# Score tiles of three attention layers laid out by source, from broadcast rows

## The chip, the cores and the metric

The kernel runs on one core of one Trainium2 chip. The metric is the device time of one execution in microseconds, lower is better; a quoted time is the median of a few runs. TensorE (PE) multiplies matrices and writes PSUM; VectorE (DVE), ScalarE (ACT) and GpSimd (POOL) work on elements; each engine runs its own instructions in order and they wait for each other on semaphores.

## The reference

Four graph networks run one after another over 625 nodes with 768 features, each followed by a residual layer norm: an RGCN (three layers), a GCN (two), a GAT with 4 heads and then 1, and a GAT with 8 heads of 96 features and then 1. What matters here is the attention layer, computed for each head:

```python
h = (x @ W).reshape(n, heads, out_c)
al_s = jnp.einsum('nhc,hc->nh', h, a_src)
al_d = jnp.einsum('nhc,hc->nh', h, a_dst)
e = jax.nn.leaky_relu(al_s[src] + al_d[dst], 0.2)
m = jax.ops.segment_max(e, dst, num_segments=n)
ex = jnp.exp(e - m[dst])
z = jax.ops.segment_sum(ex, dst, num_segments=n)
alpha = ex / (z[dst] + 1e-16)
out = jax.ops.segment_sum(h[src] * alpha[:, :, None], dst, num_segments=n)
```

## The kernel before, in words

The graph is held dense: a 625 x 625 table of edge counts in five blocks of 125 nodes (NB = 5, BP = 125). For a head, the exponent of an edge from s to d is the larger of two sums, a steep one al_s + al_d - m and a flat one 0.2 al_s + 0.2 al_d - m; m is the largest score of destination d. The four attention layers are Q0 (4 heads, a residual product beside it), Q1 (1 head, a residual product), Q2 (8 heads) and Q3 (1 head). The order of the work on each engine is written out by hand.

Each layer starts with its feature product x @ W on TensorE in chunks (`first_piece`, then `chunks_and_scores`, which calls `chunk_step` L2387 once a step and puts the score work between the steps by the table `rows_at` and `turned_at`). `early_scores` and `turn_scores` give al_s and al_d of all heads. Then, for each head:

- TensorE broadcasts al_s as one row to 125 partitions of PSUM (`send_row`, matmuls at L2457), and ScalarE copies it, times 0.8, to SBUF (`keep_row`, L1075).
- VectorE finds m for five blocks of destinations (`largest`, L1815; it waits for the copy) and makes two columns a block (`columns`, L1824 to L1827), destinations on the partitions.
- VectorE makes a 125 x 625 tile with destinations on the partitions, max(0.8 al_s + row_steep, row_flat), by `steep_or_flat` (L1885), one for each block of destinations.
- TensorE turns the five 125 x 125 blocks of the tile into PSUM (`turn_tile`, L2475), four blocks to a bank; ScalarE takes exp in place with 0.2 al_s as bias (`exps`, L1087); VectorE caps at 1 and multiplies by the counts (`probs`, L1848).
- TensorE sums the features of the sources with these blocks as stationary operand (`sum_unit`, L2486); the last column of the features is one and gives z.

In Q2 the loop runs over 40 tiles (head, block of destinations): TensorE turns tile j + 2, sums tile j and sends the row of head h + 2 when the block is 0. After a head VectorE scales its output by 1 / z and adds the bias (`head_read`, L1963 and L1967), ScalarE takes exp for the elu (`elu_exp`, L1244) and VectorE finishes the elu (`head_elu`, L1973, L1974). In Q1 four of five tiles are turned between chunk steps 4 to 7. In Q3 they are turned after the chunks. The weight chunks of the next product are split in two parts by ScalarE (L1065) and GpSimd (L766) on the way.

Of the kernel before, what the change touches and what calls it, by code (L numbers as in the profile page):

```python
# [5 lines left out]
F32 = mybir.dt.float32  # L6
# [67 lines left out]
class Attention:  # L74


    def __init__(self, before, heads, c, k, pieces, residual, chunk, loops, rows, turned, kept):
# [32 lines left out]
        self.rows_at, self.turned_at, self.kept_after = rows, turned, kept  # L110
# [15 lines left out]
        self.p_ring = {0: 4, 1: 5, 2: 6, 3: 5}[self.index]  # L126
        self.g_ring = {0: 2, 1: 3, 2: 3, 3: 3}[self.index]
# [65 lines left out]
class Memory:  # L193


    def __init__(self, nc):
# [56 lines left out]
        def edge(name, shape, dt, offset):  # L253
# [107 lines left out]
def program(nc, x, src, dst, etype, weights, rgcn_bias, gcn_bias, vec, out):  # L361
    ctx = ExitStack()
    with ctx:
# [167 lines left out]
        cols_ready = sem("cols_ready")  # L531
        g_ready = sem("g_ready")
# [32 lines left out]
        def kept_row(q, h):  # L565

            return mem.tiles[0:BP, 1 + h % 4, :]

        def g_tile(q, j):

            return mem.tiles[0:BP, {0: 5, 1: 2, 2: 5, 3: 2}[q.index] + j % q.g_ring, :]

        def p_tile(q, j):

            i = j % q.p_ring
            if q.index == 0:
                return mem.tiles[0:BP, (7, 8, 9, 0)[i], :]
            if q.index == 2:
                return mem.more[0:BP, i, :]
            return mem.tiles[0:BP, 5 + i, :]  # L580
# [111 lines left out]
        def _(pool):  # L692
# [174 lines left out]
            split_to(Q2.chunk + 15)  # L867
            split_to(Q2.end + AHEAD)
# [9 lines left out]
        def _(act):  # L878
# [190 lines left out]
            def keep_row(q, h):  # L1069

                act.wait_ge(row_sent, q.head0 + h + 1)
                if h >= 4:
                    act.wait_ge(g_ready, q.tile0 + (h - 3) * NB)
                a = row_col(q)
                nc.scalar.activation(kept_row(q, h), ps[0:BP, a:a + N], ACT.Copy, scale=1.0 - SLOPE).then_inc(row_kept, 1)  # L1075
# [15 lines left out]
            def feature_product(q):  # L1091
                n = len(q.pieces)
                for g, bank_ in enumerate(q.banks[0:NB * n]):
# [25 lines left out]
                    if m == NB - 1 and piece in q.kept_after:  # L1119
                        for step, heads, tiles in q.kept_after[piece]:  # L1120
                            split_hi(q.chunk + q.k + step + 7)
                            for h in heads:
                                keep_row(q, h)
                            exps(q, tiles)
# [93 lines left out]
            exps(Q1, NB)  # L1218
# [27 lines left out]
            for j in range(len(Q2.tiles)):  # L1246
                h, b = Q2.tiles[j]
                split_hi(min(chunks_split[0] + 1, Q2.end + AHEAD))
                exps(Q2, min(j + 3, len(Q2.tiles)))
                if b == 0 and h + 2 < Q2.heads:  # L1250
                    keep_row(Q2, h + 2)
                if b == 3 and h:
                    elu_exp(h - 1)
            elu_exp(Q2.heads - 1)
# [4 lines left out]
            exps(Q3, NB)  # L1259
# [8 lines left out]
        def _(dve):  # L1268
# [527 lines left out]
            def scores_begin(q):  # L1796
# [5 lines left out]
                                             ALU.mult))  # L1802
                if q.index + 1 < len(LAYERS):
                    scores_split(q.index + 1)

            def largest(q, h, m):

                mask = mem.mask_loop if q.loops else mem.mask_plain
                if m == 0:
                    dve.wait_ge(row_kept, q.head0 + h + 1)  # L1810
# [40 lines left out]

            def inverse(z, sums, guard):
# [25 lines left out]
            def steep_or_flat(q, j):  # L1878

                h, b = q.tiles[j]  # L1880
                dve.wait_ge(cols_ready, q.head0 + h + 1)
                dve.wait_ge(row_kept, q.head0 + h + 1)
                if j >= q.g_ring:
                    dve.wait_ge(g_turned, (q.tile0 + j - q.g_ring + 1) * NB)
                nc.vector.tensor_scalar(g_tile(q, j), kept_row(q, h), mem.row1[0:BP, b, h:h + 1], mem.row2[0:BP, b, h:h + 1],  # L1885
# [804 lines left out]
```

## Time and profile before

| what | us |
|---|---|
| median of 3 runs | 1610.96 (1610.59 to 1614.87) |
| profiled execution | 1607.97 |
| its span | 1606.2 |
| PE busy | 1464.7 (91%) |
| DVE busy | 791.7 (49%) |
| ACT busy | 427.4 (27%) |
| POOL busy | 506.6 (32%) |

The span is from the first to the last instruction in the trace. Times in the rows are counted from its start. The attention layers begin near 1000 us: Q1's scores stand at 1212 to 1248, Q2's at 1353 to 1506, Q3's at 1534 to 1594.

### The profile page before, as it was taken

The numbers are of one execution on the slowest core, as the hardware profiler recorded it, in microseconds if no ns is written. First come the engines' busy times: TensorE is split into PE (matmuls) and PEld (weight loads), VectorE is DVE, ScalarE is ACT, GpSimd is POOL, SyncE is SP. The second block draws the span as 40 slices with busy tenths as digits, with TensorE's granted clock in tenths as the row PEclk, the third lists the DMA queues.
The fourth block names the chain that finished last, engine by engine and source line by source line (L and its number), as shares of the span: only waits on it lengthen the run. The fifth ranks groups of instructions, "written<-read, shape, count | busy, mean of one in ns | idle before, by whom it ended". The sixth has DMA issues, their size and how long they took to land.

```text
span 1606.2 us, 23414 instructions
## 1 busy us (share of the span) xinstructions
PE 1464.7 (91%) x8072; PEld 1343.7 (84%) x8072; DVE 791.7 (49%) x1940; ACT 427.4 (27%) x1009; POOL 506.6 (32%) x586
## 2 busy tenths in 40 slices
PE   5899699999999999999999998999688998878896
PEld 3566699999999999999998997898578867767773
DVE  7889644224443365642324435534534043678524
ACT  1153511111000001101003113345524333544422
POOL 5110332423334424434342420633226534100020
PEclk9999899999999999999999998999889999777998
DMA  3110111213343243422112211310012102000001
GB/s 113 41 30 9 37 45 30 60 32 82 89 132 105 63 116 84 123 74 60 55 50 59 60 30 41 87 58 26 20 47 81 49 5 84 16 1 1 10 1 48
DMA packets 57656, 86.53 MB, mean 54 GB/s; under 512 B 6442, under 2 KB 54183, under 8 KB 57433
## 3 DMA queue, kind: packets, MB, share of 16 engines
q1 hardware_dynamic: 45184, 66.02, 14.3%
q10 hardware_dynamic: 12374, 19.17, 4.1%
q8 instruction: 66, 1.08, 0.3%
q14 instruction: 32, 0.26, 0.1%
HBM read 83.24 MB, written 1.92 MB: 53 GB/s over the span
## 4 chain that ended last, share of the span: by engine, by line
PE 74%; DVE 14%; ACT 5%; issue 4%; POOL 1%; DMA 1%; DVEq 0%; ACTq 0%; SPq 0%; POOLq 0%
PE psum L2060 13%; PE psum L2064 12%; PE psum L2063 12%; PE psum L2486 7%; PE psum L2077 7%; PE psum L2080 7%; PE psum L2165 2%; PE psum L2401 1%; PE psum L2406 1%; PE psum L2405 1%; ACT psum L1087 1%; DVE onehot_dst L1370 1%; PE psum L2121 1%; PE psum L2475 1%; PE psum L2457 1%
## 5 line engine op out<-in xcount | busy, mean ns | idle before, releaser
L2060 PE MATMUL psum<-w_lo,xT_hi 128*125 128x384 f32 (+2 forms) x1200 | 412.1, 343 | 11.7 <-POOL w_lo L766 5.3
L2063 PE MATMUL psum<-w_hi,xT_lo 128*125 128x384 f32 (+2 forms) x1200 | 405.5, 338 | 0.0
L2064 PE MATMUL psum<-w_hi,xT_hi 128*125 128x384 f32 (+2 forms) x1200 | 405.0, 337 | 0.0
L753 POOL CAST w_hi<-w_raw 128x384 fp32r<-128x384 f32 x190 | 103.3, 544 | 502.4 <-PE psum L2064 492.3
L2060 PEld LDWEIGHTS psum<-w_lo,xT_hi 128*125 128x125 f32 (+1 forms) x1200 | 225.0, 187 | 16.5 <-POOL w_lo L766 8.3
L766 POOL TENSOR_TENSOR w_lo<-w_raw,w_hi 128x384 fp32r<-128x384 f32 x106 | 109.8, 1065 | 387.9 <-ACT w_hi L1065 277.1
L2063 PEld LDWEIGHTS psum<-w_hi,xT_lo 128*125 128x125 f32 (+1 forms) x1200 | 225.4, 188 | 0.1
L2064 PEld LDWEIGHTS psum<-w_hi,xT_hi 128*125 128x125 f32 (+1 forms) x1200 | 224.8, 187 | 0.0
L1406 DVE TENSOR_TENSOR h_lo<-psum,h_hi 125x384 fp32r<-125x384 f32 (+1 forms) x120 | 66.9, 558 | 316.1 <-ACT h_hi L923 315.1
L2077 PE MATMUL psum<-h_lo,adjacency 125*125 125x384 f32 (+3 forms) x600 | 204.1, 340 | 1.8 <-ACT adjacency L963 1.7
L755 POOL TENSOR_TENSOR w_lo<-w_raw,w_hi 128x384 fp32r<-128x384 f32 x190 | 200.8, 1057 | 15.2
L923 ACT ACTIVATE h_hi<-psum 125x384 fp32r<-125x384 f32 (+1 forms) x120 | 59.0, 491 | 545.3 <-PE psum L2064 540.9
L2080 PE MATMUL psum<-h_hi,adjacency 125*125 125x384 f32 (+3 forms) x600 | 203.4, 339 | 0.0
L2486 PE MATMUL psum<-features,score_tiles 125*125 125x257 f32 (+2 forms) x400 | 122.6, 461 | 4.4 <-DVEq L2012 3.1
L2077 PEld LDWEIGHTS psum<-h_lo,adjacency 125*125 125x125 f32 (+1 forms) x600 | 112.0, 187 | 3.2 <-ACT adjacency L963 2.3
L1087 ACT ACTIVATE psum<-psum,al_src_slope 125x125 f32<-125x125 f32 x350 | 94.7, 351 | 73.9 <-PE psum L2475 73.8
L2080 PEld LDWEIGHTS psum<-h_hi,adjacency 125*125 125x125 f32 (+1 forms) x600 | 112.5, 188 | 0.3
L2486 PEld LDWEIGHTS psum<-features,score_tiles 125*125 125x125 f32 x400 | 79.2, 202 | 36.6 <-issue 5.0
L2486 PE MATMUL psum<-features,more_tiles 125*125 125x97 f32 x400 | 68.5, 334 | 26.1 <-DVE more_tiles L1848 25.9
L2486 PEld LDWEIGHTS psum<-features,more_tiles 125*125 125x125 f32 x400 | 63.5, 246 | 30.1 <-DVE more_tiles L1848 30.0
L2165 PE MATMUL psum<-onehot_dst,onehot_src 128*125 128x512 bf16 x336 | 62.5, 326 | 6.3 <-DVE onehot_dst L1370 5.9
L1370 DVE TENSOR_SCALAR onehot_dst<-iota,dst_of_pair 128x625 bf16<-128x625 f16 x168 | 62.8, 410 | 9.7 <-PE psum L2165 9.7
(286 smaller groups left out, 2097.9 us busy)
## 6 DMA issues: line engine op xcount, KB each, us to landing
w_raw<-weights_dram SPq DMA_DIRECT2D x296, 192.0 KB, 2.4
score_w_raw<-weights_dram ACTq DMA_DIRECT2D x58, 192.0 KB, 2.9
x_nat<-x_dram SPq DMA_DIRECT2D x1, 1875.0 KB
x_residual<-x_dram SPq DMA_DIRECT2D x1, 1875.0 KB
out_dram<-x_residual SPq DMA_DIRECT2D x5, 375.0 KB
score_a_rows<-L_gnn_a_src_dram ACTq DMA_DIRECT2D x8, 192.0 KB, 3.4
score_a_rows<-L_gnn_a_dst_dram ACTq DMA_DIRECT2D x8, 192.0 KB, 5.1
rgcn_bias<-rgcn_bias_dram SPq DMA_DIRECT2D x1, 1125.0 KB
```

Source lines behind the costliest of these rows:

```text
L753: nc.gpsimd.tensor_copy(mem.wh[:, slot, :], mem.raw[:, raw_slot, :]).then_inc(w_hi_ready, 1)
L755: nc.gpsimd.tensor_tensor(mem.wl[:, slot, :], mem.raw[:, raw_slot, :], mem.wh[:, slot, :].bitcast(F32), ALU.subtract).then_inc(w_lo_ready, 1)
L766: nc.gpsimd.tensor_tensor(mem.wl[:, c % WRING, :], mem.raw[:, c % RAW, :], mem.wh[:, c % WRING, :].bitcast(F32), ALU.subtract).then_inc(w_ ...
L1087: ins = nc.scalar.activation(t, t, ACT.Exp, bias=mem.al_src2[0:BP, n % NB, h:h + 1])
L1370: nc.vector.tensor_scalar(mem.oh_dst[:, n % OH_RING, 0:N], mem.iota[:, 0:N], mem.dst_pair[:, s % 2, j:j + 1], None, ALU.is_equal).then_inc ...
L2060: ins = nc.tensor.matmul(o, h, wl, start=(j == 0), stop=False, skip_group_check=True)
L2063: nc.tensor.matmul(o, l, wh, start=False, stop=False, skip_group_check=True)
L2064: ins = nc.tensor.matmul(o, h, wh, start=False, stop=stop and j == k - 1, skip_group_check=True)
L2077: ins = nc.tensor.matmul(o, a, mem.hl[0:p, slot, 0:width], start=(s == 0), stop=False, skip_group_check=True)
L2080: ins = nc.tensor.matmul(o, a, mem.hh[0:p, slot, 0:width], start=False, stop=(s == NB - 1), skip_group_check=True)
L2165: ins = nc.tensor.matmul(o, mem.oh_src[:, t, 0:BP], mem.oh_dst[:, n % OH_RING, w:w + 512 if w == 0 else NC], start=False, stop=(t == GROUP ...
L2486: ins = nc.tensor.matmul(bank(q.out_bank(u), off, off + width), blocks(p_tile(q, j))[:, k, :], feat_flat(q, k, a, a + width), start=(k == ...
```

## The change

Q0 stays as it is. In Q1, Q2 and Q3 the tiles have sources on the partitions and destinations along the free dimension, so that no block has to be turned. What changes:

- `keep_row` is gone in these layers; `largest` waits for the row in PSUM.
- `turn_columns`: after `columns`, TensorE turns the two columns of each of five blocks (125 x 2) into two rows of 625 in PSUM. `keep_columns`: ScalarE copies the two rows to SBUF in two instructions.
- `send_columns`: TensorE broadcasts the flat row and then the steep row to 125 partitions of PSUM, 2 x 2 pieces. `keep_flat`: ScalarE copies the flat one to SBUF.
- `score`: VectorE makes each of five 125 x 625 tiles as max(steep row + 0.8 al_s, flat row) with the steep row in PSUM and the flat one in SBUF. `source_exps`: ScalarE takes exp of a whole tile in SBUF. `finish`: VectorE caps at 1 and multiplies by the counts, all in SBUF.
- `sum_head` (Q2): all five tiles of a head are used together, 25 blocks of 97 columns, as each tile becomes ready.
- In Q2, scaling a head's output by 1 / z goes to ScalarE (five instructions on 96 columns) and adding the bias to GpSimd; the loop runs over heads and TensorE's order in it is `turn_columns(h+1)`, `send_columns(h+1)`, `send_row(h+2)`, `sum_head(h)`. The turn stands before chunk step 3 and the send before step 4 in all three layers; the row of head 1 of Q2 moves from step 4 to step 5 and waits for head 0's tiles to be scored, since it shares their bank. GpSimd splits one weight chunk fewer before Q2's heads.

The core of the diff:

```diff
 Q1 = Attention(Q0, 1, D, K8, PIECES, True, BASE_L2B, True,
-               {1: (0,)}, {4: 0, 5: 1, 6: 2, 7: 3}, {0: ((1, (0,), 0), (5, (), 2), (7, (), 4))})
+               {1: (0,)}, {3: ("turn", 0), 4: ("send", 0)}, {0: ((3, (0,), 0), (6, (), NB))})
 Q2 = Attention(Q1, HEADS3, C3, KC, PIECES, False, BASE_L3, False,
-               {1: (0,), 4: (1,)}, {}, {0: ((1, (0,), 0), (4, (1,), 0))})
+               {1: (0,), 5: (1,)}, {3: ("turn", 0), 4: ("send", 0)}, {0: ((3, (0,), 0), (4, (), NB))})
 Q3 = Attention(Q2, 1, D, KC, PIECES, False, BASE_L3 + 2 * KC, False,
-               {1: (0,)}, {}, {0: ((1, (0,), 0),)})
+               {1: (0,)}, {3: ("turn", 0), 4: ("send", 0)}, {0: ((3, (0,), 0), (4, (), NB))})
...
+            def keep_columns(q, h):
+                act.wait_ge(cols_turned, q.head0 + h - HEADS2 + 1)
+                if q.by_head and h >= 2:
+                    act.wait_ge(pair_sent, q.head0 + h - HEADS2 - 1)
                 a = row_col(q)
-                nc.scalar.activation(kept_row(q, h), ps[0:BP, a:a + N], ACT.Copy, scale=1.0 - SLOPE).then_inc(row_kept, 1)
+                nc.scalar.activation(kept_columns(h)[:, 0:4 * BP], ps[0:2, a:a + 4 * BP], ACT.Copy)
+                nc.scalar.activation(kept_columns(h)[:, 4 * BP:N], ps[0:2, a + 512:a + 512 + BP], ACT.Copy).then_inc(cols_kept, 1)
+            def keep_flat(q, h):
+                if apart(q, h):
+                    act.wait_ge(flat_sent, h)
+                else:
+                    act.wait_ge(pair_sent, q.head0 + h - HEADS2 + 1)
+                a = pair_col(q, h, 1)
+                nc.scalar.activation(flat_row(h), ps[0:BP, a:a + N], ACT.Copy).then_inc(flat_kept, 1)
+            def source_exps(q, h):
+                for k in range(NB):
+                    t = source_tile(q, h, k)
+                    act.wait_ge(tile_scored, scored(q, h, k))
+                    nc.scalar.activation(t, t, ACT.Exp, bias=mem.al_src2[0:BP, k, h:h + 1]).then_inc(tile_exp, 1)
...
+            for h in range(HEADS3):
+                if h + 1 < HEADS3:
+                    keep_columns(Q2, h + 1)
+                    keep_flat(Q2, h + 1)
+                if h:
+                    head_read(h - 1)
+                if h + 1 < HEADS3:
+                    source_exps(Q2, h + 1)
+                if h:
                     elu_exp(h - 1)
...
+            def score(q, h, k):
+                if k == 0:
+                    dve.wait_ge(pair_sent, q.head0 + h - HEADS2 + 1)
+                    dve.wait_ge(flat_kept, q.head0 + h - HEADS2 + 1)
+                    if q.by_head and h >= 2:
+                        dve.wait_ge(part_done, q.unit0 + h - 1)
+                nc.vector.scalar_tensor_tensor(source_tile(q, h, k), steep_row(q, h), mem.al_steep[0:BP, k, h:h + 1], flat_row(h),
+                                               ALU.add, ALU.max).then_inc(tile_scored, 1)
+            def finish(q, h, k):
+                cnt, t = mem.cnt_loop if q.loops else mem.ctot, source_tile(q, h, k)
+                dve.wait_ge(tile_exp, scored(q, h, k))
+                nc.vector.scalar_tensor_tensor(t, t, 1.0, cnt[0:BP, k, 0:N], ALU.min, ALU.mult).then_inc(tile_ready, 1)
...
+            scores_of(Q2, 0)
+            for k in range(NB):
+                score(Q2, 0, k)
+            for h in range(HEADS3):
+                if h + 1 < HEADS3:
+                    scores_of(Q2, h + 1)
+                for k in range(NB):
+                    finish(Q2, h, k)
+                if h:
+                    head_z(h - 1)
+                if h >= 2:
+                    head_elu(h - 2)
+                if h + 1 < HEADS3:
+                    for k in range(NB):
+                        score(Q2, h + 1, k)
...
+            scores_of(Q3, 0)
+            for step in (score, finish):
+                for k in range(NB):
+                    step(Q3, 0, k)
...
+            def turn_columns(q, h):
+                pe.wait_ge(cols_ready, q.head0 + h + 1)
+                for m in range(NB):
+                    a = row_col(q) + (m * BP if m < NB - 1 else 512)
+                    ins = nc.tensor.transpose(ps[0:2, a:a + BP], mem.row12[0:BP, :, m, h], mem.ident[0:BP, 0:BP])
+                ins.then_inc(cols_turned, 1)
+            def send_columns(q, h):
+                pe.wait_ge(cols_kept, q.head0 + h - HEADS2 + 1)
+                if h:
+                    pe.wait_ge(tile_scored, scored(q, h - 1, NB - 1))
+                    if h == 1:
+                        pe.wait_ge(gemm_read, q.gemm0 + NB + 2)
+                for i in (1, 0):
+                    for p, e, a, z in score_pieces(pair_col(q, h, i)):
+                        ins = nc.tensor.matmul(ps[0:BP, p:e], mem.ident[0:2, i:i + 1].to_broadcast([2, BP]),
+                                               kept_columns(h)[:, a:z], start=True, stop=True)
+                    if i and apart(q, h):
+                        ins.then_inc(flat_sent, 1)
+                ins.then_inc(pair_sent, 1)
...
+            for h in range(HEADS3):
+                if h + 1 < HEADS3:
+                    turn_columns(Q2, h + 1)
+                    send_columns(Q2, h + 1)
+                if h + 2 < HEADS3:
                     send_row(Q2, h + 2)
+                sum_head(h)
```

## Rows read from the trace of the kernel before

**Rows 1.** Windows: length, busy us (count) of each engine, granted clock, DMA.

```profile
core 0: us, PE busy (x) PEld busy (x) DVE busy (x) ACT busy (x) POOL busy (x), PEclk, DMA share, GB/s
1379.00:1442.00 63.00, 49.93 (x273) 44.52 (x274) 44.62 (x117) 27.58 (x97) 0.00 (x0) 0.74 0.00 1
1442.00:1506.00 64.00, 52.81 (x338) 49.42 (x336) 50.27 (x128) 31.48 (x110) 0.00 (x0) 0.80 0.00 1
...
1379.00:1382.00 3.00, 2.63 (x11) 2.46 (x12) 0.77 (x3) 0.94 (x4) 0.00 (x0) 0.50 0.00 0
...
1393.00:1400.00 7.00, 6.58 (x49) 5.50 (x48) 3.47 (x13) 5.03 (x19) 0.00 (x0) 1.00 0.00 0
...
1573.00:1576.00 3.00, 2.91 (x5) 1.62 (x6) 2.68 (x8) 0.20 (x1) 0.00 (x0) 0.57 0.00 0
```

**Rows 2.** Waits over the span: who waited for whom, total us, times, longest.

```profile
DVE max_scratch L1815 <- ACT score_tiles L1075: 44.1, 13, 5.2
```

**Rows 3.** Instruction groups by shape in Q2's loop, 1379.4 to 1505.4 us.

```profile
L2486 PE MATMUL psum<-features,more_tiles 125*125 125x97 f32 x400 | 68.5, 334 | 26.1 <-DVE more_tiles L1848 25.9
...
L1815 DVE CUSTOM_DVE_ANT_0 max_scratch<-psum,mask_plain 125x625 f32<-125x625 f32 x30 | 24.1, 803 | 22.9 <-ACT score_tiles L1075 22.7
L1885 DVE TENSOR_SCALAR score_tiles<-score_tiles,row_steep,row_flat 125x625 f32<-125x625 f32 x35 | 21.0, 599 | 0.2 <-PE psum L2475 0.2
L1848 DVE SCALAR_TENSOR_TENSOR more_tiles<-psum,counts_all 125x500 f32<-125x500 f32 x19 | 12.7, 670 | 0.8 <-ACT psum L1087 0.5 <-PE psum L2486 0.3
...
L1963 DVE TENSOR_TENSOR residual_product<-psum,z 125x480 f32<-125x480 f32 x7 | 4.6, 658 | 0.2
L1974 DVE SCALAR_TENSOR_TENSOR residual_product<-residual_product,elu_exp 125x480 f32<-125x480 f32 x7 | 4.6, 658 | 0.2
...
L1075 ACT ACTIVATE score_tiles<-psum 125x625 f32<-125x625 f32 x6 | 4.2, 692 | 11.3 <-PE psum L2457 11.3
L1973 DVE TENSOR_SCALAR elu_exp<-elu_exp 125x480 f32<-125x480 f32 x7 | 2.8, 406 | 3.4 <-ACT elu_exp L1244 3.4
```

**Rows 4.** Page, costliest groups: ScalarE's exp and GpSimd's chunk split.

```profile
L766 POOL TENSOR_TENSOR w_lo<-w_raw,w_hi 128x384 fp32r<-128x384 f32 x106 | 109.8, 1065 | 387.9 <-ACT w_hi L1065 277.1
...
L1087 ACT ACTIVATE psum<-psum,al_src_slope 125x125 f32<-125x125 f32 x350 | 94.7, 351 | 73.9 <-PE psum L2475 73.8
```

**Rows 5.** Timeline of DVE: first and last instruction of head 1's maxima and columns.

```profile
1369.86 0.81 DVE L1815 CUSTOM_DVE_ANT_0 max_scratch<-psum,mask_plain 125x625 f32<-125x625 f32 x1 [2.65 <-ACT score_tiles L1075]
...
1374.61 0.16 DVE L1827 SCALAR_TENSOR_TENSOR row_flat<-al,al_max 125x5 f32<-125x5 f32 x1
```

**Rows 6.** Chain of waits in Q2: start us, length us, engine and line.

```profile
1358.50 1.25 PE psum L2457 x4
...
1381.79 2.41 PE psum L2457 x4
...
1396.18 0.57 PE psum L2475 x5
1396.75 1.07 PE psum L2486 x10
...
1507.98 0.67 DVE residual_product L1974
```

**Rows 7.** Chain of waits and timelines of PE and DVE in Q1's scores.

```profile
1218.55 1.27 PE psum L2457 x4
...
1225.98 1.77 DVE L1826 TENSOR_TENSOR row_steep<-al,al_max 125x5 f32<-125x5 f32 x1
...
1230.03 0.81 PE L2475 MATMUL psum<-ident,score_tiles 125*125 125x125 f32 x5 [2.11 <-DVE score_tiles L1885]
```

**Rows 8.** Chain of waits in Q3: its row, its first two and its last sums.

```profile
1538.18 1.25 PE psum L2457 x4
...
1555.76 6.72 PE psum L2486 x20
...
1573.09 21.32 PE psum L2486 x60
```

More of the change, by code:

```diff
@@ L148, in turns_within, with pair_bank @@
         return self.turns if tiles == len(self.tiles) else tiles * NB // 4
+    def pair_bank(self, h):
+        return 5 if self.residual else 4 if self.by_head and h else 2
     def out_bank(self, u):
@@ L1244, in elu_exp, with head_read @@
                 nc.scalar.activation(mem.elu[0:BP, h % 2, :, :], strip(h), ACT.Exp).then_inc(elu_out, 1)
[L1246 to L1252, printed above, removed]
+            def head_read(h):
+                act.wait_ge(z_ready, len(Q0.units) + NB + h + 1)
+                for m in range(NB):
+                    ins = nc.scalar.activation(strip(h)[:, m, :], head_out(h)[:, m, 0:C3], ACT.Copy,
+                                               scale=mem.z[0:BP, m, h % 2:h % 2 + 1])
+                ins.then_inc(part_read, 1)
+            for h in range(HEADS3):
[7 more added lines that the diff above has]
+                if h:
                     elu_exp(h - 1)
-            elu_exp(Q2.heads - 1)
+                split_hi(min(chunks_split[0] + 3, Q2.end + AHEAD))
+            head_read(HEADS3 - 1)
+            elu_exp(HEADS3 - 1)
             for m in range(NB):
@@ L1802, in scores_begin @@
                                              ALU.mult))
+                if q.index:
+                    link(nc.vector.tensor_scalar(mem.al_steep[0:BP, :, 0:q.heads], mem.al[0:BP, :, 0:q.heads], 1.0 - SLOPE, None,
+                                                 ALU.mult))
                 if q.index + 1 < len(LAYERS):
@@ L1889, in _ @@
             for h in range(HEADS2):
-                for m in range(NB):
-                    largest(Q0, h, m)
-                columns(Q0, h)
+                scores_of(Q0, h)
             for j in range(3):
@@ L1935, in _ @@
             scores_begin(Q1)
-            for m in range(NB):
-                largest(Q1, 0, m)
-            columns(Q1, 0)
-            for j in range(NB):
-                steep_or_flat(Q1, j)
-            probs(Q1, NB)
+            scores_of(Q1, 0)
+            for step in (score, finish):
+                for k in range(NB):
+                    step(Q1, 0, k)
             for s in range(NB + 2):
@@ L2015, in _ @@
             scores_begin(Q3)
-            for m in range(NB):
-                largest(Q3, 0, m)
-            columns(Q3, 0)
-            for j in range(NB):
-                steep_or_flat(Q3, j)
-            probs(Q3, NB)
+            scores_of(Q3, 0)
+            for step in (score, finish):
+                for k in range(NB):
+                    step(Q3, 0, k)
             for s in range(NB):
@@ L2597, in _ @@
             chunks_and_scores(Q2, mem.xh, mem.xl)
[L2598 to L2605 removed]
+            for h in range(HEADS3):
+                if h + 1 < HEADS3:
+                    turn_columns(Q2, h + 1)
+                    send_columns(Q2, h + 1)
+                if h + 2 < HEADS3:
                     send_row(Q2, h + 2)
+                sum_head(h)
             def turn_q2(m):
```

200 lines of the change are left out of this document (107 added, 93 removed).

## The prediction

> **What bounds the kernel now.** I read the windows first [rows 1]. In Q2's loop over heads (1379 to 1506 us) no engine is full: TensorE is busy 103 of 127 us, but at a granted clock of 0.74 and 0.80, and VectorE 95 of 127. At full clock TensorE's work is small: ten sum instructions (one tile) take 1.07 us, five turns 0.57, a row 1.25 [rows 6], so a head takes 5 x (1.07 + 0.57) + 1.25 = 9.5 us of some 17 from one head to the next. The groups of the loop [rows 3] give VectorE's work and what it waits for: 22.9 of its idle us come before the maxima, which wait for ScalarE's copy of the row; over the span that wait is 44.1 us [rows 2]. TensorE in turn waits 26 us for VectorE's finished tiles [rows 3]. So the loop is a cycle of waits between the two engines, with VectorE carrying most of it, and its gaps pull TensorE's clock down: 0.50 behind a wait, 1.00 once it has streamed [rows 1]. The loop ends with the elu at 1508.6 [rows 6]; I count it from head 0's row, sent at 1359.75 (1358.50 + 1.25) [rows 6]: 148.9 us. Q1's and Q3's tiles sit in TensorE's path with one short wait each [rows 7, 8].
>
> **Q2, VectorE.** Maxima and columns of a head stay: 1369.86 to 1374.77 is 4.9 us [rows 5]. Taken away are five steep_or_flat (0.60), the probs (500 columns in 0.67, ten instructions) and two 480-column steps of head_read (0.66) [rows 3]. Added are 5 `score` and 5 `finish`, each scalar_tensor_tensor over 625 columns. Such an instruction takes 0.67 for 500 columns from PSUM and 0.66 for 480 in SBUF [rows 3], and the maximum 0.80 for 625 [rows 3], so I take 0.81 long and, as they overlap a little when queued (the maxima start 0.85 apart with an accumulator read of 0.08 between), 0.73 apart. Bounds: 0.60 (the tensor_scalar row) and 1.0 (0.66 x 625/480 plus 0.15 for the column operand). A head then costs 4.95 + 3.65 + 3.65 + 0.4 (1/z) + 1.05 (elu, 0.41 + 0.66 and a link) = 13.7 us.
>
> The row on steep_or_flat bears on a rule. It takes 0.60 for 625 columns where the 480-column two-tensor steps take 0.66 [rows 3]. The Trainium skill, VectorE: DVE Perf Modes (section "Mode 2×_2P"), says that an fp32 tensor_scalar in SBUF may run two elements a cycle while an instruction with a second tensor, or a PSUM operand, may not. It speaks against this change: `score` gives that mode up. The trace agrees in direction only, 0.60 to 0.81 and not a doubling; by the rule in full each score would cost 0.4 more than the old instruction ought to, 2 us a head.
>
> **Q2, the chain of a head.** With C the end of columns(h+1): five column turns 0.6 (as the turns of 125 columns, 0.57 [rows 6]), ScalarE's two small copies 0.8 (the 625-column copy is 0.69 [rows 3], twice a fixed part; bounds 0.5 and 1.4), two rows 2 x 1.27, with hops of 0.1: the pair is there at C + 4.3. VectorE has `finish`, 1/z and elu until C + 5.1, so at full clock the chain is hidden and the cycle is 13.7 us. `send_row` of the next head ends at C + 5.6, before VectorE wants it at C + 8.8; the wait of 3.8 us a head is gone. ScalarE has 0.8 + 0.7 + 1.4 (five 96-column reads; 0.35 for 125 [rows 4], overlapping) + 3.4 (five exps, each taken as the 625-column copy, 0.69 [rows 3]) + 0.65 = 7 us, hidden. The bias add on GpSimd, idle in the loop, is 1.2 (1.07 for 384 columns [rows 4]), hidden until the last head.
>
> But the clock will not be full. The sums of a head end at about C + 11, then TensorE waits 2.8 us for columns, turns, and waits 0.9 for the copies. Waits of 2 to 3 us before did bring 0.50 [rows 1]. At 1.2 GHz a row takes 2.41 [rows 6]: turns to C + 1.2, copies to 2.1, pair at C + 7.0, so `score` runs from C + 7.1 to 10.8 and the cycle is 10.8 + 4.9 = 15.7. The sums then run mostly at full clock, ending by C + 15. I take 15.4, near the low-clock end since the pause recurs with each head.
>
> Start: VectorE ends columns(0) 5.05 after the row. TensorE ends chunk steps 1 and 2 (2.7 each) at 5.4, turns by 6.1, step 3 to 8.8, pair by 11.4, flat copied at 12.1, scored at 15.9. Row 1 shares the bank and waits for that: sent at 17.2 (before: 9.3), so columns(1) end at 22.2 where they ended at 15.0 [rows 5]. That is 7 us given back. Then six cycles of 15.4 = 92.4, then the last two heads without maxima: finish, score, finish, sums to 15.5, and a serial tail of 1/z, ScalarE 1.4, GpSimd 1.2, exp 0.6, elu 1.1, together 22. Sum 22.2 + 92.4 + 22 = 136.6 against 148.9: Q2 gains 12.3 us.
>
> **Q1.** Before, TensorE turned at step 4 and waited 2.11 us [rows 7]; having done steps 1 to 3 from 1219.8 to 1227.9, 2.7 us each; now it must turn the columns before step 3, 2.7 us earlier, while the columns come only 0.7 earlier (no copy of the row). VectorE's small steps are slow there (row_steep 1.77 us [rows 7] where it is 0.2 in Q2), GpSimd being busy. Columns at 1228.1, steps 1 and 2 over at 1225.2: a wait of 2.9. Turns and two rows, 3.3 us, replace five tiles turned at 0.6 to 0.8 each (3.2). Net 1.6 later (0.8 more wait, the rest from the tighter end of the chunks); if the wait drops the clock, up to 3 more. I take +2.5, bounds 0 and +6. The tiles then have over 25 us of residual product as cover, so `score` and `finish` cost nothing, even slowed by GpSimd to 1 us each. If that cover were gone they would cost 8 us.
>
> **Q3.** The row is sent at 1539.4 [rows 8]. No wait at the turn (columns at +5.05, steps to 5.4), pair at +11.4, chunks done at +16.8 = 1556.2 (before 1552.8). Scores to +15.9, finish to +19.7, and `sum_tile` waits for all five tiles: 1559.2, a wait of 3. Then the sums, five times 6.5 (6.72 for the first with its start [rows 8]), and 1.6 for the clock behind the wait, as it was 0.57 behind the wait at 1573 [rows 1]: end 1593.3 where they ended at 1594.4 (1573.09 + 21.32 [rows 8]). Q3 gains 1.0, bounds -3 and +3.
>
> **Sum.** +2.5 - 12.3 - 1.0 = -10.8 on the profiled execution's 1607.97 (span 1606.2) = 1597.2. The median of the runs lies 3.0 above the profiled one: **1600**.
>
> **Rivals.**
> A, clock stays full in Q2's loop. Cycle 13.7: 22.2 + 82.2 + 20.7 = 125.1, gain 24, Q1 +1.6, Q3 -2.5: 1586. For it: the clock was 1.00 over a whole stretch of sums, turns and a row [rows 1], and a head now has one long pause where it had several. Against: that pause recurs each head.
> B, the clock recovers late. Broadcasts from two partitions may not bring it up, so part of the sums runs at 1.2 GHz too: turns, copies and both rows 7.0, next row 2.4, sums half slow 8 = 17.4, and VectorE no longer decides. The loop then takes 22.2 + 6 x 17 + 22.5 = 146.7, gain 2; Q1 +4.5, Q3 0: 1613. For it: clocks of 0.50 over whole tiles [rows 1].
> C, slower than before: the same mechanism further. If three quarters of a head's sums run at 1.2 GHz the cycle is 9.4 + 9.4 = 18.8; loop 22.2 + 113 + 24 = 159, +10, with Q1 +4.5: 1625. It decides from the point where over half of the sums are slow, since (148.9 - 44.7) / 6 = 17.4. For it: per head TensorE issues 8 more broadcast instructions, in a row, all behind a wait. All at 1.2 GHz would give a cycle of 20.5.
> D, the change doesn't do what it says, because start and tail (44 us) eat what the cycles give: VectorE at 1.0 a tile makes the cycle 16.4 and the loop 143, gain 6: 1607.
>
> **Numbers.** Forecast 55%, A 10%, B 13%, C 12%, D 10%. What a measurement can tell from no change is 0.3%, 4.8 us. Faster is the forecast, A and part of D: 0.68. Same: B and the rest of D, 0.20. Slower: C, 0.12. Range 1587 to 1614: A's end below, B above; C is left out. The forecast's own range is 1594 to 1607.
>
> **What would show it.** Right: a cycle of 14.5 to 16 us in Q2 between rows, `score` and `finish` near 0.8, no wait for a copied row, a broadcast pair of about 4.8 us at clock 0.50 and sums at 1.00; head 1's row 17 us after head 0's; one 3 us wait before Q3's sums; a wait near 2.9 in Q1. Wrong: cycles over 17, sums of 2.4 us a tile, tiles of 1.0 us or ScalarE on the path.

## The result, and the profile after

The changed kernel takes 1592.99 us (median of 4 runs, 1592.07 to 1593.48) where the kernel before takes 1610.96 (1610.59 to 1614.87): 0.9882 of it, with a 95% interval of 0.9865 to 0.9899. The forecast was 1600, its own range 1594 to 1607 and the whole range 1587 to 1614: the result lies in the whole range and 1 us below the forecast's own. The profiled execution took 1592.07 (span 1590.3) where the one before took 1607.97 (span 1606.2): -15.9.

Windows of the loop over heads in Q2 and of Q3 after its pair, in the trace after (columns as in [rows 1]):

```profile
1383.00:1438.00 55.00, 51.72 (x248) 40.66 (x247) 51.67 (x109) 28.93 (x56) 4.88 (x5) 0.72 0.03 8
1438.00:1494.00 56.00, 48.89 (x281) 41.99 (x280) 44.94 (x94) 24.82 (x54) 6.96 (x6) 0.77 0.00 1
...
1391.00:1397.00 6.00, 6.00 (x24) 4.86 (x23) 5.93 (x10) 4.33 (x6) 0.00 (x0) 0.50 0.01 3
1398.00:1404.00 6.00, 5.18 (x37) 3.96 (x36) 5.31 (x15) 1.28 (x3) 0.00 (x0) 1.00 0.00 0
...
1537.50:1540.50 3.00, 3.00 (x10) 3.00 (x11) 2.27 (x3) 1.98 (x3) 0.00 (x0) 0.50 0.00 0
```

Against [rows 1] the reader sees two things. In the first window both engines are now nearly full: VectorE 51.7 of 55 us where it was 44.6 of 63, TensorE 51.7 of 55 (the second window holds the loop's tail). And TensorE's clock is no better than before, 0.72 and 0.77. The stretches at 0.50 have changed their nature: TensorE is busy 6.00 of 6.00 us in one and 3.00 of 3.00 in the other.

Instruction groups of the loop after (columns as in [rows 3]):

```profile
L2638 PE MATMUL psum<-features,more_tiles 125*125 125x97 f32 x240 | 40.4, 348 | 0.0
...
L2638 PE MATMUL psum<-features,score_tiles 125*125 125x97 f32 x160 | 23.7, 321 | 0.0
...
L1903 DVE CUSTOM_DVE_ANT_0 max_scratch<-psum,mask_plain 125x625 f32<-125x625 f32 x35 | 28.3, 808 | 2.9 <-PE psum L2554 1.9
...
L1954 DVE SCALAR_TENSOR_TENSOR more_tiles<-more_tiles,counts_all 125x625 f32<-125x625 f32 x24 | 18.0, 805 | 0.0
L2575 PE MATMUL psum<-score_tiles,ident 2*125 2x512 f32 x28 | 15.9, 648 | 5.7 <-ACT score_tiles L1127 5.7
L1947 DVE SCALAR_TENSOR_TENSOR more_tiles<-psum,al_src_steep,score_tiles 125x625 f32<-125x625 f32 x19 | 15.4, 862 | 4.5 <-PE psum L2575 4.3
L1143 ACT ACTIVATE more_tiles<-more_tiles,al_src_slope 125x625 f32<-125x625 f32 x19 | 15.0, 817 | 3.1 <-DVE more_tiles L1947 2.8
```

The 22.9 us of idle time before the maxima [rows 3] are 2.9 now, and the wait for a copied row [rows 2] is gone. `finish` (L1954) takes 0.80 and `score` (L1947) 0.86; the 26 us that TensorE idled before the sums [rows 3] are 0.0.

One head in the timeline of TensorE, then of VectorE (start us, length us; the bracket is idle time before it and its releaser):

```profile
1404.33 2.33 PE L2554 MATMUL psum<-score_tiles,ident 16*125 16x512 f32 x4
1406.59 2.42 PE L2638 MATMUL psum<-features,more_tiles 125*125 125x97 f32 x10
1408.80 5.66 PE L2638 MATMUL psum<-features,score_tiles 125*125 125x97 f32 x40
1414.30 0.70 PE L2563 MATMUL psum<-ident,row_steep_flat 125*2 125x125 f32 x5
1415.82 2.52 PE L2575 MATMUL psum<-score_tiles,ident 2*125 2x512 f32 x8 [0.82 <-ACT score_tiles L1127]
1418.13 2.33 PE L2554 MATMUL psum<-score_tiles,ident 16*125 16x512 f32 x4
```

```profile
1413.20 0.17 DVE L1915 SCALAR_TENSOR_TENSOR row_steep_flat<-al,al_max 125x5 f32<-125x5 f32 x1
1413.28 3.68 DVE L1954 SCALAR_TENSOR_TENSOR more_tiles<-more_tiles,counts_all 125x625 f32<-125x625 f32 x5
...
1417.58 0.66 DVE L2075 SCALAR_TENSOR_TENSOR residual_product<-residual_product,elu_exp 125x480 f32<-125x480 f32 x1
1418.37 0.87 DVE L1947 SCALAR_TENSOR_TENSOR more_tiles<-psum,al_src_steep,score_tiles 125x625 f32<-125x625 f32 x1
```

The columns are ready at C = 1413.37. TensorE turns them only at C + 0.93, when its sums end, and its one pause is 0.82. The pair (L2575) is sent at full clock, 2.52 long; right behind it the row takes 2.33, and behind the pair before it the row took 2.33 and the first ten sums 2.42, the lengths of 1.2 GHz. Then the clock is back. The pair is there at C + 5.0, VectorE's elu ends at C + 4.9: two chains end together.

The chain of waits after, with Q1's row, at Q2's start, at its end, and in Q3, answering to [rows 6], [rows 7] and [rows 8]:

```profile
1220.13 1.27 PE psum L2554 x4
...
1363.79 0.37 PE psum L2494
...
1494.14 0.67 DVE residual_product L2075
...
1525.17 1.25 PE psum L2554 x4
...
1535.07 2.34 PE psum L2575 x8
...
1545.86 32.58 PE psum L2604 x100
```

From head 0's row to the end of the last elu Q2's loop takes 1363.79 to 1494.8 = 131.0 us, 148.9 before: a gain of 17.9. Q3, from its row (1526.42) to the end of its sums (1578.4), takes 52.0 where it took 1539.4 to 1594.4 = 55.0: a gain of 3.0. Ahead of Q2's loop 4.0 were lost (1359.75 to 1363.79), and they fall into two parts. Q1's row ended at 1221.40 where it ended at 1219.82 [rows 7]: 1.6 us were lost before it, in work that the change leaves as it was (one and the same matmul starts at 522.6 and at 524.3). From Q1's row to Q2's it took 142.4 where it took 139.9: a loss of 2.5. Between Q2's loop and Q3's row 0.8 were lost. Together 1.6 + 2.5 - 17.9 + 0.8 - 3.0 = -16.0, against -15.9 for the spans. Where the 1.6 come from stays open: in the other traces below, q1_later aside, Q1's row ended 0.4 to 2.6 us later than in the one before, with nearly the same code ahead of it.

### The profile page after: what moved, and what is told of

Its sections match the earlier page's. It is cut to its first block, busy times and chain, and to the rows that moved or that the text cites. A ratio compares the mean times of both kernels' runs of the same rounds, so it can differ in the third digit from the quotient of the medians.

```text
span 1590.3 us, 22908 instructions
## 1 busy us (share of the span) xinstructions
PE 1467.6 (92%) x7952; PEld 1334.0 (84%) x7952; DVE 794.0 (50%) x1877; ACT 416.3 (26%) x869; POOL 516.1 (32%) x594
## 4 chain that ended last, share of the span: by engine, by line
PE 77%; DVE 13%; ACT 4%; issue 3%; POOL 1%; DMA 1%; ACTq 0%; DVEq 0%; SPq 0%; POOLq 0%
PE psum L2153 13%; PE psum L2156 13%; PE psum L2157 13%; PE psum L2170 7%; PE psum L2173 7%; PE psum L2604 5%; PE psum L2638 3%; PE psum L2258 2%; PE psum L2575 2%; PE psum L2494 2%; PE psum L2499 1%; PE psum L2498 1%; DVE onehot_dst L1453 1%; PE psum L2554 1%; PE psum L2214 1%
## 5 line engine op out<-in xcount | busy, mean ns | idle before, releaser
L1667 DVE CUSTOM_DVE_ANT_0 score_products<-score_w_raw,score_a_rows 128x384 f32<-128x384 f32 (+2 forms) x116 | 57.2, 538 | 12.5 <-DMA score_w_raw<-weights_dram 9.1
L1967 DVE RECIPROCAL z<-psum 125x1 f32<-125x1 f32 x25 | 4.2, 168 | 118.4 <-PE psum L2604 118.4
L2258 PEld LDWEIGHTS psum<-onehot_dst,onehot_src 128*125 128x125 bf16 x336 | 38.7, 144 | 29.0 <-issue 20.5
```

The source lines that it names most:

```text
L2258: ins = nc.tensor.matmul(o, mem.oh_src[:, t, 0:BP], mem.oh_dst[:, n % OH_RING, w:w + 512 if w == 0 else NC], start=False, stop=(t == GROUP ...
```

## The experiments

Twelve kernels ran, in three groups on three chips, each beside the kernel before. Below, "loop" is in the profiled execution from the first maximum of Q2's head 0 to the last elu's end (before 148.0, after 131.0), "cycle" the mean from one head's first maximum to the next over heads 1 to 7 (before 16.7, after 13.9), "Q1" the time from Q1's first maximum to Q2's (before 140.0, after 142.4). The ratio is to the kernel before on the same chip. The diffs are shortened, and the comments in them are this text's.

```
kernel        median   ratio   95% interval        Q1     loop   cycle
after         1592.99  0.9882  0.9865 to 0.9899   142.4  131.0  13.9
after_again   1595.45  0.9920  0.9892 to 0.9948   142.2  132.6  14.5
elu_pool      1597.06  0.9921  0.9890 to 0.9951   144.0   133.7  14.4
sends_wide    1594.76  0.9896  0.9869 to 0.9923   141.8   131.5  14.5
less_sum      1590.96  0.9872  0.9844 to 0.9899   144.0   127.4  14.0
elu_less      1593.27  0.9894  0.9863 to 0.9924   142.3   132.3  13.9
q1_later      1597.30  0.9909  0.9882 to 0.9936   141.7  137.4  15.2
q1_quiet      1592.01  0.9881  0.9852 to 0.9910   138.8  136.0  14.7
fill_narrow   1593.49  0.9906  0.9868 to 0.9943   142.5  133.9  14.3
wide_fill     1582.27  0.9824  0.9802 to 0.9847   141.5  122.1  13.3
quiet_fill    1579.45  0.9807  0.9789 to 0.9826   136.6  124.8  13.8
best          1580.12  0.9814  0.9793 to 0.9836   136.6  124.0  12.8
b_head_read   1609.75  1.0001  0.9981 to 1.0020   140.0   146.7  16.1
```

**after_again**, the changed kernel once more, as the measure for the others.

> The changed kernel itself, beside the others of this group. It gave 1593.0 us. Its loop of the second of the three layers (from its row sent to the last elu) took 131.0 us in the one execution profiled, the stretch between the second layer's first maximum and the third's 142.4. Every theory expects 1591 to 1595 us again; it shows how far the loop's length (cycles of 13.2 to 15.2, by where the low clock falls) moves from one execution to the next with nothing changed: if it moves by more than 3 us, then the loops of the runs so far (127.4 to 137.4) can't be compared one by one, and their times must be.

1595.45, just above what was expected; the loop moved by 1.6 us. The same kernel's ratio came out at 0.988 and at 0.992, so nothing between these two counts as a gain or a loss, and of the table only the three kernels below 1583 us are apart from the changed one. The loop of one profiled execution says less still: q1_later and q1_quiet have the changed kernel's loop unedited, and it took 137.4 and 136.0 there.

**b_head_read**, the kernel before with one part of the change alone: the reading of a finished head on ScalarE and the bias on GpSimd.

```diff
 # GpSimd, at the end of its work
+nc.gpsimd.tensor_tensor(t, t, b, ALU.add).then_inc(elu_in, 1)   # bias, per head
 # ScalarE, in Q2's loop of tiles
+if b == 2 and h: head_read(h - 1)      # five activations, scale=z
 # VectorE
-head_read(h - 1)                        # product and bias, 480 columns each
+head_z(h - 1)                           # 1/z only
```

> The kernel before, with one part of the change alone: the scaling of a head's output by 1 / z on ScalarE and the bias on GpSimd instead of two VectorE steps (1.3 us a head) in Q2. If VectorE's load set the old cycle of 17 us, Q2's loop falls by 8 us (148.0 to 140). If the chain of waits (row sent behind a sum, copied, then the maxima, which interleave with the tiles) set it, by 0 to 4 us; the rest of the gain is then the new layout.

The loop took 146.7 against 148.0, the time is the same. VectorE had 1.3 us a head less to do and waited longer: the wait before the maxima grew from 22.9 to 24.9 in the loop.

```profile
L1832 DVE CUSTOM_DVE_ANT_0 max_scratch<-psum,mask_plain 125x625 f32<-125x625 f32 x30 | 24.1, 804 | 24.9 <-ACT score_tiles L1081 24.7
```

The cycles fell by 0.6 us, to 16.1, and of the 3.4 us that this gave up to head 7's first maximum the loop's tail took 2.1 back, where ScalarE and GpSimd stand in a row behind the last sums. So VectorE's load didn't set the old cycle, and the gain of the change is in the new layout and not in this part. That the chain row, copy, maxima set it is read from the waits [rows 3]; the opposite test, maxima in the old kernel that wait only for the row in PSUM, wasn't run. So how much of the gain comes from the missing copy, and how much from the turns that TensorE no longer does, isn't shown.

**elu_pool**: VectorE relieved. The elu of heads 0 to 5 goes to GpSimd.

```diff
+nc.gpsimd.tensor_scalar(e, e, 1.0, -1.0, ALU.min, ALU.add)
+nc.gpsimd.tensor_scalar(t, t, 0.0, None, ALU.max).then_inc(pool_elu_done, 1)
+nc.gpsimd.tensor_tensor(t, t, e, ALU.add).then_inc(layer_ready, 1)
 # VectorE
-if h >= 2: head_elu(h - 2)
```

> The kernel after, with the elu of heads 0 to 5 of Q2 (two VectorE steps, 1.05 us a head) moved to GpSimd, which idles there. Its cycle of heads is 13.2 to 15.3 us. Theory V, VectorE's load sets the cycle: each of six cycles falls by about 1 us, Q2's loop from 131.0 to about 125 us, time 1587. Theory P, TensorE with its stretches at 1.2 GHz sets the cycle (13.8 us of turns, copies, sends, row and sums, end to end): no change, within 1 us of 1593.

No gain: 1597.06, loop 133.7. Theory V's 1587 didn't come: VectorE's load alone isn't what bounds the head.

**less_sum**: TensorE relieved. The kernel leaves out four of 25 sum matmuls of each head.

```diff
-for b in range(NB):
+for b in range(NB if k < NB - 1 else 1):     # Q2 only
```

> The kernel after, with four of 25 sum matmuls of each head of Q2 left out (sources 500 to 624 are summed for the first block of destinations only), which takes 0.9 us a head from TensorE at full clock and 1.8 at 1.2 GHz and nothing from VectorE. Theory P: six cycles fall by 1 to 1.8 us, time 1583 to 1587. Theory V: only the last head's sums are shorter, about 1 us, time 1592.

The loop is 3.6 us shorter, less than the loops of the same code differ by; the time, 1590.96, isn't told apart from 1592.99, and theory P's 1583 to 1587 didn't come.

**elu_less**: both together.

> elu_pool and less_sum together (the elu of heads 0 to 5 on GpSimd, and four of 25 sum matmuls of each head of Q2 left out). Each alone left the usual cycle near 13.8 us. Theory: two paths of the same length set it, VectorE's load (13.7) and the chain columns, turn, copy, send, score, maxima, which TensorE enters 0.9 us late behind its sums; with both relieved the cycle is 12.7 to 13.2 and Q2's loop about 123 to 125 us. Rival, something else sets 13.6 to 13.8 (ScalarE, a fixed part of the chain): cycles as in less_sum, loop 127.

Its theory, cycles of 12.7 to 13.2, didn't come: they were 13.2 to 15.3, four of the six 13.6 to 13.7, with both engines relieved, and the loop 132.3. Why is in one head, TensorE and then VectorE:

```profile
1437.07 5.67 PE L2650 MATMUL psum<-features,score_tiles 125*125 125x97 f32 x32
1442.58 0.70 PE L2575 MATMUL psum<-ident,row_steep_flat 125*2 125x125 f32 x5
1444.10 2.41 PE L2587 MATMUL psum<-score_tiles,ident 2*125 2x512 f32 x8 [0.82 <-ACT score_tiles L1140]
```

```profile
1446.54 0.87 DVE L1960 SCALAR_TENSOR_TENSOR more_tiles<-psum,al_src_steep,score_tiles 125x625 f32<-125x625 f32 x1 [1.01 <-PE psum L2587]
```

The columns ended at 1441.63, and the turn again came only at the end of the sums, 0.95 later. 32 sums at full clock take 3.6 us (1.14 for ten); here 5.67. The low clock, which comes within or behind every pair of the loop, eats what fewer sums save. VectorE now waits 1.01 for the pair. So the clock is the question, and what brings it down.

**sends_wide**: the pair broadcast from 125 partitions, of which 123 hold zeros.

```diff
-nc.tensor.matmul(ps[0:BP, p:e], mem.ident[0:2, i:i + 1].to_broadcast([2, BP]),
-                 kept_columns(h)[:, a:z], start=True, stop=True)
+nc.tensor.matmul(ps[0:BP, p:e], mem.ident[0:BP, i:i + 1].to_broadcast([BP, BP]),
+                 mem.tiles[0:BP, 10 + h % 2, a:z], start=True, stop=True)
```

> The kernel after, with the pair of rows broadcast from 125 partitions (123 of them zero) instead of from 2; same number of TensorE instructions and columns; one GpSimd clear of 0.8 us before Q1. In the trace of after the granted clock falls from 1.00 to 0.50 right behind these sends in most heads and in Q3's chunks, where TensorE had not paused. Theory P with the two-partition sends as the cause of the low clock: granted clock stays 1.00 behind them, the sums of a head take 5.4 to 6 us instead of 7.8 to 9.4, the two cycles of 15 us go to 13.8 or less and Q3 gains 1.6: time 1587 to 1590. Theory that the pauses of 0.82 us or the loop's cadence lower the clock: no change, 1593.

Behind the sends of heads 1 and 5, which went at full clock, it stayed at 1.00, and the 50 sums took 5.70 where they take 7.3 to 9.4 in the changed kernel where the clock falls. But then they end early, TensorE pauses for the columns, and the next pair is sent at 1.2 GHz, on the path:

```profile
1421.15 5.70 PE L2642 MATMUL psum<-features,more_tiles 125*125 125x97 f32 x50
1428.85 0.69 PE L2567 MATMUL psum<-ident,row_steep_flat 125*2 125x125 f32 x5 [2.00 <-DVE row_steep_flat L1919]
1430.37 4.59 PE L2579 MATMUL psum<-score_tiles,ident 125*125 125x512 f32 x8 [0.82 <-ACT score_tiles L1131]
```

This is the mechanism of the forecast, pause and slow pair, and five of its six cycles are 14.4 to 15.5. The time stayed. (GpSimd's clear took 1.14 us, where 0.8 was expected.)

**wide_fill** and **fill_narrow**: matmuls whose output nobody reads fill the pauses before the pairs of heads 2 to 7, with the wide pair and with the pair of the change (narrow, from two partitions).

```diff
+def keep_warm(h, n):       # into the bank of this head's sums, before they begin
+    for _ in range(n):
+        nc.tensor.matmul(bank(Q2.out_bank(h), 0, HW), mem.xh[:, 0, nodes(0)],
+                         mem.xl[:, 0, 0:HW], start=True, stop=True, ...)
...
+    if h: keep_warm(h, 8)
     turn_columns(Q2, h + 1)
+    if h: keep_warm(h, 4)
     send_columns(Q2, h + 1)
```

> sends_wide plus matmuls whose result nobody reads: 8 of 384 columns (1.4 us) before each column turn of Q2's heads 2 to 7 and 4 (0.7 us) between turn and send, in the time in which TensorE waits anyway. In sends_wide the clock stayed 1.00 behind the sends, the sums took 5.70 us instead of 7.8, but TensorE then paused 2.0 us, and the next sends ran at 1.2 GHz (4.59 us instead of 2.41), on the path. Theory: with the pauses filled the clock stays 1.00 over the loop, every send takes 2.4 us, cycles are 13.6 to 13.8 and the loop about 127 to 128 us against 131.5. Rival, the fill delays the turn more than the clock gives: cycles over 14.4.

> The changed kernel with the filler matmuls alone (8 of 384 columns before a head's columns are turned and 4 between turn and send, heads 2 to 7), the pair still broadcast from two partitions. Theory P (TensorE's clock falls because of the broadcasts from two partitions, 2.4 us of them, and the row's from sixteen): the clock is again seen to fall right behind the sends, cycles of 13.6 to 15.5, 1588 to 1595 us. Theory I (it falls because of TensorE's idle time within a head, some 3 us, and the kind of send is of no matter): the filler closes that, the clock stays at 1.00 and the time is that of the run with both, 1582 us, cycles of 13.6.

The same 90 us of the loop, 1390 to 1480, in fill_narrow and then in wide_fill:

```profile
1390.00:1480.00 90.00, 89.24 (x491) 75.57 (x490) 80.88 (x169) 42.94 (x87) 7.09 (x6) 0.81 0.00 1
```

```profile
1390.00:1480.00 90.00, 82.55 (x565) 68.07 (x566) 87.50 (x180) 47.93 (x95) 7.37 (x7) 1.00 0.00 1
```

This pair of runs settles that the narrow pair brings the clock down. With filler and the narrow pair TensorE is busy 89.24 of 90 us and its clock is still 0.81. With filler and the wide pair it is busy less, 82.55, with pauses of up to 1.36 us before a turn, at 1.00, and the time falls to 1582.27. Neither edit alone moved the time measurably.

All the traces together say the same. In the eight kernels with the narrow pair, 52 pairs of the loop's heads 1 to 7 were sent at full clock, and each time the clock fell, between 2.4 us before the pair's end and 2.6 us behind it. In the four with the wide pair 35 were sent at full clock, and it fell at one, 0.2 us into it and behind a pause of 2.00 (sends_wide). The narrow pairs that stand among the chunks (Q1, Q2's head 0, Q3) brought it down in 10 of 24 cases only; what tells these from the others wasn't tested. In the changed kernel the clock stayed up behind Q1's pair and fell behind Q3's:

```profile
1235.20 2.32 PE psum L2575 x8
...
1236.00:1242.00 6.00, 6.00 (x33) 5.32 (x32) 3.63 (x5) 4.41 (x7) 2.98 (x3) 1.00 0.13 35
```

VectorE then goes from elu (ends 1416.44) to `score` without a gap:

```profile
1415.78 0.66 DVE L2079 SCALAR_TENSOR_TENSOR residual_product<-residual_product,elu_exp 125x480 f32<-125x480 f32 x1
1416.35 0.86 DVE L1951 SCALAR_TENSOR_TENSOR more_tiles<-psum,al_src_steep,score_tiles 125x625 f32<-125x625 f32 x1
```

Its load is the bound: 13.57 to 13.58 in the four cycles that hold an elu, 12.8 in the two that don't; the prediction had 13.7.

**q1_later** and **q1_quiet**, on Q1's wait: the turn a step later, or GpSimd's five additions of 125 x 768 (L874) held back until the columns are made.

```diff
-{3: ("turn", 0), 4: ("send", 0)}, {0: ((3, (0,), 0), (6, (), NB))}
+{4: ("turn", 0), 5: ("send", 0)}, {0: ((4, (0,), 0), (6, (), NB))}
```

```diff
+split_to(Q1.chunk + 18)
+pool.wait_ge(cols_ready, Q1.head0 + 1)
 for m in range(NB):
-    split_to(Q1.chunk + 12 + m)
     skip_row(m)
```

> The kernel after, with Q1's turn of the columns before chunk step 4 and the send before step 5 instead of 3 and 4. Theory: Q1's 4.0 us of loss are the wait of 3.5 us before the turn and the 3.4 us at 1.2 GHz behind it; one step later the columns have been ready for 0 to 1 us wait, the clock stays full, and 3.5 to 5 us come back: time 1588 to 1589.5. Rival: the loss is in the later end of scores, features and weight splits, then the same or more is lost behind the chunks: time 1593 or above.

> The kernel after, with GpSimd's five skip_row additions (1.83 us each) of Q1 held back until Q1's columns are made, where they fall into GpSimd's idle time. In after, VectorE's four small steps behind the maxima take 4.6 us beside these additions and 0.7 us in Q2, and TensorE waits 3.5 us for them and then runs 3 us at 1.2 GHz. Theory: they take 0.7 us, the wait all but goes, the clock stays 1.00 and 4 to 5 us of the profiled time come back: from Q1's first maximum to Q2's, 142.4 us in after, it is 137.5 to 138.5. Rival, the small steps are slow for another reason (the chunk splits beside them): less than 1 us.

VectorE's small steps and TensorE's wait behind them in the changed kernel:

```profile
1225.68 0.96 DVE L1912 TENSOR_TENSOR al_sum<-al_max,al 125x5 f32<-125x5 f32 x1
1226.68 0.92 DVE L1913 SCALAR_TENSOR_TENSOR al_max<-al_sum 125x5 f32<-125x5 f32 x1
1227.63 1.72 DVE L1914 TENSOR_TENSOR row_steep_flat<-al,al_max 125x5 f32<-125x5 f32 x1
1229.27 1.03 DVE L1915 SCALAR_TENSOR_TENSOR row_steep_flat<-al,al_max 125x5 f32<-125x5 f32 x1
...
1230.36 1.20 PE L2563 MATMUL psum<-ident,row_steep_flat 125*2 125x125 f32 x5 [3.50 <-DVE row_steep_flat L1915]
```

and the first and third of these steps in q1_quiet, where TensorE turns without a wait:

```profile
1224.72 0.17 DVE L1913 TENSOR_TENSOR al_sum<-al_max,al 125x5 f32<-125x5 f32 x1
...
1225.13 0.17 DVE L1915 TENSOR_TENSOR row_steep_flat<-al,al_max 125x5 f32<-125x5 f32 x1
```

GpSimd's work beside them made four steps of 0.17 take 0.9 to 1.7 each. It was additions and chunk splits in turn, and the 0.92 step stood beside a split alone; in q1_quiet GpSimd was idle during all four, so the two aren't told apart. q1_later missed: with this work still there the columns came later too, and TensorE still waited 2.4. In q1_quiet the stage is 3.6 us shorter, a little under the expected 4 to 5, but this execution's loop took 136.0, with the low clock in worse places, and the median didn't move. What Q1 gives is kept only where the clock is held:

**quiet_fill** and **best**: q1_quiet's and wide_fill's edits together, and with elu_pool's as well.

> The changed kernel with three edits: the pair broadcast from 125 partitions, the filler matmuls, and GpSimd's five skip rows held back until the first layer's columns are made. Without the last of the three it gave 1582.3 us, and alone the last took 3.6 us off the first stage. If the stages are independent: 1582.3 - 3.6 = 1578.7, range 1577 to 1581, with cycles of 13.6 as before. Rival: what the first stage gains is given back in the second (as in the run of that edit alone, 1592.0 against 1593.0), 1581 to 1583.

> The kernel with those three edits and the elu of heads 0 to 5 on GpSimd as well, which takes 1.03 us a head off VectorE (0.38 and 0.66 in the rows of the run with both clock edits) and nothing off TensorE. Theory V (with the clock held at 1.00, VectorE's load of 13.6 us a head is the bound): cycles of 12.6 to 13.1, 5 us less in the loop, 1573 to 1576 us. Theory S (TensorE's sums, filler and sends bound the head, VectorE's load beside them is a coincidence): cycles stay at 13.4 to 13.6, 1578 to 1580 us. Without the clock edits the same move gave nothing (1597.1 against 1593.0).

quiet_fill: 1579.45, near the sum; its interval (0.9789 to 0.9826) still overlaps that of wide_fill. In best the six cycles were 12.80 to 12.82, as theory V had it: with the clock held, 1.03 us off VectorE gave 0.76 in a head whose cycle had been 13.57. Yet the time, 1580.12, is that of quiet_fill, and not theory V's 1573 to 1576. The end of the loop, GpSimd and then VectorE:

```profile
1473.24 1.82 POOL L919 TENSOR_SCALAR elu_exp<-elu_exp 125x480 f32<-125x480 f32 x1
1475.03 1.41 POOL L920 TENSOR_SCALAR residual_product<-residual_product 125x480 f32<-125x480 f32 x1
1476.53 1.20 POOL L922 TENSOR_TENSOR residual_product<-residual_product,elu_exp 125x480 f32<-125x480 f32 x1
1477.68 1.20 POOL L928 TENSOR_TENSOR residual_product<-residual_product,par 125x480 f32<-125x480 f32 x1
```

```profile
1472.55 0.19 DVE L1985 RECIPROCAL z<-z 125x5 f32<-125x5 f32 x1
1477.76 1.39 DVE L2092 TENSOR_SCALAR elu_exp<-elu_exp 125x480 f32<-125x480 f32 x1 [5.01 <-POOL residual_product L922]
```

The last head's 1/z was ready at 1472.7, 4.3 earlier than in quiet_fill (1477.0), but its bias waited on GpSimd behind the elu of head 5. From head 7's first maximum to the last elu it took 29.0 us against 25.1: 3.9 of the 5.8 that the heads had gained (2.7 of these in one cycle that had held the low clock in quiet_fill); 1.1 more went in head 0's cycle, where the low clock fell. Moving only the first heads' elu might keep them; it wasn't run.

## Why the prediction was right, step by step

The sign and the stage held, and so did the main reading: a head bound by the wait for the copied row became one in which VectorE hardly waits. What the forecast said of the clock did not: it looked for a pause and a slow pair in each head, and they came in one head only, and small (a pause of 0.54, a pair of 3.44). Of the profiled execution's -15.9 its sum, -10.8, missed 5.1: 5.6 in Q2 and 2.0 in Q3, less the 1.6 ahead of Q1's row and the 0.8 ahead of Q3's, for which it had no term. The median missed by 7.0, the other 2 of it because it lies 0.9 above the profiled execution and not 3.0 as taken. That 1600 came near is in part luck: the term of the cycles was 8.8 too long, and the longer tail and what was lost outside the three stages gave part of it back.

**Q2, -12.3 forecast, -17.9 measured.** By parts:
- Start: 22.2 forecast; columns(1) ended 22.6 after head 0's row. Right.
- VectorE's load: 0.81 long and 0.73 apart taken; `score` 0.86 and 0.79 apart, `finish` 0.80 and 0.72 apart. 13.7 a head forecast, 13.57 measured in wide_fill. Right. `score` takes 0.86 where the old tensor_scalar took 0.60, less than twice as long. The trace keeps agreeing with the Trainium skill, VectorE: DVE Perf Modes (section "Mode 2×_2P"), in direction only.
- Six cycles of 15.4 = 92.4 forecast, 83.6 measured (13.9 each). **This is the term that was mis-sized, by 8.8.** It rested on "then TensorE waits 2.8 us for columns", so that the pair would be sent at 1.2 GHz. The pause didn't come: TensorE waited for columns in one head, 0.54. In the changed kernel the clock fell at the pair's end or behind it, and so slowed the row and the sums behind it; 50 sums took 7.3 to 9.4 instead of 5.7 and ended 0.9 after the columns, and the pause was filled by slow work. The pair itself, the part on the path, went at full clock in six of the seven heads (3.44 in the other). sends_wide shows the forecast's picture where the pause does come: 2.00 us, pair 4.59, cycles up to 15.5.
- The chain was called hidden by 0.8 us at full clock (C + 4.3 against C + 5.1). It is level (C + 5.0 and C + 4.9), since the turn waits for the slow sums. That fits elu_pool, which found nothing to gain on VectorE's side.
- Tail: 22 forecast, 131.0 - 22.6 - 83.6 = 24.8 measured; the low clock falls in it too (1476 to 1483).

**Q1, +2.5 forecast, +2.5 measured** from its row to Q2's. The wait at the turn was 3.50 where 2.9 was taken; without GpSimd beside VectorE's small steps it goes (q1_quiet: 0.17 each, no wait, -3.6). The clock then fell behind the wait, named in the forecast as up to 3 more. The other 1.6 us by which Q2 began later were lost before Q1's row.

**Q3, -1.0 forecast, -3.0 measured.** The pair came 11.0 after the row (11.4 forecast), and the wait before the sums was 1.48 (3 forecast), as the chunks under it ran partly at 0.50, again right behind the pair. The sums then took 32.58 in one stretch at full clock, with no loss behind the wait; the forecast had added 1.6 for that. Here the execution was lucky: in after_again, the same kernel, the wait was 3.03 and the sums took 34.27, so Q3's gain there is 1.3 us, near the 1.0 forecast.

**Rivals.** A had the cycle (13.7) for the wrong reason: the clock was not full, 0.72. B's condition was true of the loop, and more than true: the pairs from two partitions not only don't bring the clock up, they bring it down. Its price was wrong, because it let the whole pair go slow as well. C needed over half of the sums at 1.2 GHz. In the loop's groups 400 sums took 64.1 us (40.4 and 23.7) where 40 x 1.14 = 45.6 is full clock, so about 40% of their work was slow: nearer to C's point than a 1.1% gain lets one think. D's tiles of 1.0 us didn't come.

Left open: why the low clock lasts 3.4 us behind a narrow pair in one head and 6.8 or 10.2 in others of the same execution, which moves the loop of one kernel by some us between executions.

## What to carry to other kernels

Where two engines take turns, ask of a slow clock not only how long it lasts but on which instructions it falls: here it fell on sums that ran beside VectorE's work, and at a clock of 0.72 the cycle was 13.9, against 13.57 with the clock held; in heads where the pair itself went slow the cycles were 14.4 to 15.5 (sends_wide). What the clock cost in the kernel before, no run shows. A broadcast by matmul from two partitions takes no longer than one from 125 (2.4 us for the pair), and can be dear by the clock behind it; widening the operand with zeros and filling the pauses are worth trying together, since neither alone moved the time by what could be measured, and both together took the ratio from 0.988 to 0.982 (wide_fill, 0.9802 to 0.9847). Work moved to an idle engine is free only until the last item: look at what queues behind it at the end of the loop.

## What the runs showed of the hardware that was not expected

- TensorE's granted clock fell from 1.00 to 0.50 within 2.6 us behind 2.4 us of fp32 broadcasts from 2 partitions, or in their second half, in all 52 such pairs of the loop, with TensorE busy throughout in fill_narrow (89.24 of 90 us at a clock of 0.81); in 10 of 24 among the chunks, so in the changed kernel's Q3, where no pause stood near (1537.5 to 1540.5: busy 3.00 of 3.00 at 0.50). The same broadcasts from 125 partitions, 123 of them zeros, left it at 1.00 (wide_fill), though the next head's row still came from 16 partitions. They took the same 2.4 us.
- VectorE's steps over 125 x 5 elements took 0.92 to 1.72 us while GpSimd added 125 x 768 tiles or split 128 x 384 chunks, 0.17 with GpSimd idle.
- In best, beside GpSimd's bias addition and a chunk split, VectorE's elu steps of 480 columns took 1.39 and 1.33, alone 0.40 and 0.66.
- GpSimd, 125 x 480 fp32: 1.82 for a tensor_scalar with two operations, 1.41 with one, 1.20 for a tensor_tensor (up to 1.74 and 1.53 for the last two in single cases of best).
